# Four buffers instead of two and three between VectorE and the adding transfers of the last stage

## What is computed

```python
gate_scores = jax.nn.sigmoid(xf @ gate_w.T + balance_bias)
topk_scores, topk_idx = jax.lax.top_k(gate_scores, 2)          # 2 of 8 experts for each token
topk_scores = topk_scores / (topk_scores.sum(axis=-1, keepdims=True) + 1e-06)
comb = zeros((T, 8)).at[arange(T)[:, None], topk_idx].add(topk_scores)
h = jax.nn.silu(jnp.einsum('td,ehd->teh', xf, w1))              # 256 -> 512 for each expert
expert_out = jnp.einsum('teh,edh->ted', h, w2)                  # 512 -> 256
out = jnp.einsum('te,ted->td', comb, expert_out)                # weighted sum of two experts
```

## Time and profile before

| | |
|---|---|
| median of three runs | 3291.21 us (3287.84 to 3295.37) |
| the profiled execution | 3287.47 us |
| its span, first to last instruction | 3285.3 us |
| mean granted TensorE clock | 0.936 |
| busy share: TensorE, VectorE, ScalarE, GpSimd | 83%, 58%, 46%, 44% |
| the last stage | about 2958 to 3286 us |

### The profile page before, as it was taken

How to read it: one execution, slowest core, us unless ns; L and a number is a source line. 1 busy time by engine, 2 the same in 40 slices (tenths; PEclk the granted TensorE clock), 3 DMA queues, 4 the chain that set the end, 5 groups by cost and what they waited for, 6 DMA issues and landing times.

```text
span 3285.3 us, 49090 instructions
## 1 busy us (share of the span) xinstructions
PE 2739.6 (83%) x16588; PEld 1861.5 (57%) x16588; DVE 1904.1 (58%) x3444; ACT 1520.3 (46%) x2639; POOL 1452.9 (44%) x1633
## 2 busy tenths in 40 slices
PE   6888888857887888786999998799788888749997
PEld 2333333325564566533888875697555555537776
DVE  3888888866887688751222224402789998851111
ACT  4566665535775666410222210443666666522222
POOL 3666676654444577525000006300455555532333
PEclk8999999999998999988999999799999999869999
DMA  9600000000012000022566652100000000007675
GB/s 325 218 1 0 1 1 0 1 0 30 20 66 76 1 1 1 1 71 91 182 219 210 210 164 81 54 1 1 7 28 33 29 28 28 21 34 218 189 198 131
DMA packets 131956, 243.97 MB, mean 74 GB/s; under 512 B 15184, under 2 KB 103376, under 8 KB 121040
## 3 DMA queue, kind: packets, MB, share of 16 engines
q1 hardware_dynamic: 112320, 207.36, 19.4%
q0 software_dynamic: 19440, 34.10, 4.3%
HBM read 154.90 MB, written 87.43 MB: 74 GB/s over the span
## 4 chain that ended last, share of the span: by engine, by line
PE 24%; POOL 9%; issue 8%; DMA 7%; DVE 6%; ACT 2%; POOLq 1%; another core or an unknown queue 1%; SPq 0%; DVEq 0%; ACTq 0%
PE PS L2305 8%; DMA out<-f_y,f_token 6%; PE PS L1892 4%; PE PS L2261 4%; POOL e_hs L1451 2%; POOL rows_by_expert L2192 2%; POOL out L2621 1%; POOL e_qs L1454 1%; POOL rows_in_place L872 1%; PE PS L1306 1%; DVE e_mx L1354 1%; PE PS L1883 1%; PE PS L1249 1%; POOLq L2661 1%
## 5 line engine op out<-in xcount | busy, mean ns | idle before, releaser
L572 POOL TENSOR_TENSOR u_in<-dtx,b_rep 128x512 f32<-128x512 f32 x256 | 325.0, 1292 | 201.2 <-ACT b_rep L553 200.0
L588 DVE TENSOR_TENSOR_SCAN state<-PS,u_in 128x512 f32<-128x512 f32 x256 | 312.2, 1220 | 59.0 <-POOL u_in L572 34.8
L545 PE MATMUL PS<-scaled,ident 128*128 128x512 f32 x512 | 295.9, 662 | 28.2 <-DVE scaled L582 28.1
L2326 ACT ACTIVATE d_act_b<-PS 128x256 f32<-128x256 f32 (+2 forms) x192 | 76.1, 399 | 486.9 <-PE PS L2305 398.5
L1451 POOL TENSOR_TENSOR e_hs<-e_pr 128x512 f32<-128x512 f32 x128 | 162.7, 1271 | 231.0 <-ACT e_pr L1418 227.6
L2305 PE MATMUL PS<-d_unit_T,d_w 128*128 128x256 f32 (+1 forms) x1280 | 261.8, 358 | 1.0 <-ACT d_unit_T L2315 1.0
L2338 DVE TENSOR_TENSOR d_hid<-d_act_b,PS 128x256 f32<-128x256 f32 (+2 forms) x192 | 84.2, 440 | 295.9 <-ACT d_act_b L2326 276.5
L561 ACT ACTIVATE PS<-dt,decay_rate 128x508 f32<-128x508 f32 x256 | 173.5, 687 | 138.1 <-DVE state L588 136.4
L2305 PEld LDWEIGHTS PS<-d_unit_T,d_w 128*128 128x128 f32 x1280 | 222.0, 191 | 26.3 <-issue 1.4
L2621 POOL DMA_INDIRECT out<-f_y,f_token x71 | 110.2, 1553 | 218.8 <-DVE f_y L2612 160.8
L582 DVE TENSOR_TENSOR scaled<-state,PS 128x512 f32<-128x512 f32 x256 | 169.5, 665 | 55.5 <-PE PS L526 43.9
(11 more groups left out here) (451 smaller groups left out, 6477.0 us busy)
## 6 DMA issues: line engine op xcount, KB each, us to landing
d_w<-in_d_w SPq DMA_DIRECT2D x42, 1024.0 KB, 5.1
f_w<-in_f_w SPq DMA_DIRECT2D x40, 1024.0 KB, 5.1
rows_in_place<-blank SPq DMA_DIRECT2D x136, 272.0 KB, 5.0
d_w<-in_d_w SPq DMA_DIRECT2D x42, 512.0 KB, 4.0
rows_by_expert<-zeros SPq DMA_DIRECT2D x36, 256.0 KB, 2.6
f_unit_rows<-rows_in_place SPq DMA_DIRECT2D x31, 272.0 KB, 5.3
d_unit_rows<-rows_by_expert SPq DMA_DIRECT2D x31, 256.0 KB, 4.2
out_by_expert<-d_y_rows SPq DMA_DIRECT2D x31, 256.0 KB, 4.2
```

The source lines that it names most:

```text
L545: nc.tensor.matmul(YB[:, c], ident[:], scaled[:, (KD * n + c) % RC], start=False, stop=n == NS - 1).then_inc(m_y, 1)
L572: nc.gpsimd.tensor_tensor(u_in[:, k % RU], dtx[:, p, c], b_rep[:, n % RB], ALU.mult).then_inc(m_u, 1)
L588: nc.vector.tensor_tensor_scan(state[:, k % 2], DECAY[:, k % RD], u_in[:, k % RU], 0.0, ALU.mult, ALU.add).then_inc(m_h, 1)
```

## The change

`y` gets four buffers instead of two, and `token` four instead of three. The two waits on VectorE follow: both are now for the landing of unit u-4. The rings of rows and weights stay at three. No instruction is added or removed. Nothing else is touched.

```diff
--- before.py
+++ after.py
@@ -2498,7 +2498,7 @@
 
         FC, UT = 4, UR // 128
         UPS, WN = KD * 512, KD * 512 + 4 * D
-        RING = 3
+        RING, OUT = 3, 4
         mem = Stage(nc, sem_set[turn])
         t = lambda name, shape, dtype=F32: mem.take(f"{tag}_{name}", shape, dtype)
         s = lambda name: mem.sem(f"{tag}_{name}")
@@ -2508,8 +2508,8 @@
         rows = t("unit_rows", [128, RING, UT, ROW])
         xT = t("unit_T", [128, 2, KD, UR])
         hid = t("hid", [128, 2, FC, UR])
-        y = t("y", [128, 2, UT, D])
-        mine, share, token = t("mine_rows", [128, UT, E]), t("share_rows", [128, UT]), t("token", [128, RING, UT], I32)
+        y = t("y", [128, OUT, UT, D])
+        mine, share, token = t("mine_rows", [128, UT, E]), t("share_rows", [128, UT]), t("token", [128, OUT, UT], I32)
         UB = lambda f: PS[:, f, 0:UR]
         DB = lambda r: PS[:, 4 + r, 0:D]
         TB = PS[:, 6:8, 0:UR]
@@ -2601,15 +2601,15 @@
                 n = tiles[u]
                 nc.vector.tensor_tensor(mine[:, 0:n], rows[:, r, 0:n, D:D + E], table["mine"][:, u].unsqueeze(1).broadcast_to([128, n, E]),
                                         ALU.mult).then_inc(weighed, 1)
-                after(dve, added, 16 * late(u - RING + 1))
-                nc.vector.tensor_copy(token[:, r, 0:n], rows[:, r, 0:n, D + E]).then_inc(sent_to, 1)
+                after(dve, added, 16 * late(u - OUT + 1))
+                nc.vector.tensor_copy(token[:, u % OUT, 0:n], rows[:, r, 0:n, D + E]).then_inc(sent_to, 1)
                 dve.wait_ge(weighed, 2 * u + 1)
                 nc.vector.tensor_reduce(share[:, 0:n], mine[:, 0:n], AX.X, ALU.add).then_inc(weighed, 1)
                 dve.wait_ge(weighed, 2 * u + 2)
-                after(dve, added, 16 * late(u - 1))
+                after(dve, added, 16 * late(u - OUT + 1))
                 for k in range(n):
                     dve.wait_ge(down, upto[u] + k + 1)
-                    nc.vector.tensor_scalar(y[:, u % 2, k], DB(k), share[:, k:k + 1], None, ALU.mult).then_inc(mixed, 1)
+                    nc.vector.tensor_scalar(y[:, u % OUT, k], DB(k), share[:, k:k + 1], None, ALU.mult).then_inc(mixed, 1)
 
         def pool(pl):
             pl.wait_ge(stored, 16 * NG)
@@ -2618,7 +2618,7 @@
                 pl.wait_ge(sent_to, u + 1)
                 after(pl, added, 16 * upto[u])
                 for k in range(tiles[u]):
-                    nc.gpsimd.indirect_dma_start(tokens_of, bass.IndirectOffsetOnAxis(token[:, u % RING, k:k + 1], 0), y[:, u % 2, k], None,
+                    nc.gpsimd.indirect_dma_start(tokens_of, bass.IndirectOffsetOnAxis(token[:, u % OUT, k:k + 1], 0), y[:, u % OUT, k], None,
                                                  bounds_check=NG * GT - 1, oob_is_err=False, compute_op=ALU.add).then_inc(added, 16)
             pl.wait_ge(added, 16 * upto[SLOTS])
```

## The result

The changed kernel is slower: 3320.76 us (median of 4 runs, 3319.42 to 3337.45) against 3289.53 us for the kernel before (4 runs, 3280.98 to 3295.37). The ratio is 1.011, with a 95% interval of 1.008 to 1.014. The prediction was 3278 us, with a range from 3260 to 3297: the sign was wrong, and the time lies outside the range.

The account below looks back on a forecast made before the run. The prediction took the last stage's serial adding transfers, lengthened by weight loads, as the bound. Terms +3.7, -12.9 and -3.7 gave -12.9 us: 3287.47 to 3274.6, then 3.7 up to the runs' median, 3278; range 3260 to 3297.

Parts of the forecast that it names:

- The chain of landings: Last stage: each unit's adding transfers wait for the earlier landing; 0.86 us landing to issue, 1.86 more for two issues.
- The price list: GpSimd's transfers: a weight load lengthens a landing by its phase, +0.7 us at 2.8 ahead, +2.4 at 1.2 ahead.
- 164.6: Units 8 to 35: us the 21 double and 6 single units would take with no loads beside them.
- the 50.5 us: Units 8 to 35: remainder of 215.1 us beyond undisturbed transfers, claimed as the price of 27 weight loads, 1.87 each.
- the sum: Last stage: +3.7 us in units 8 to 12, -12.9 in units 12 to 33, -3.7 at the end; together -12.9.
- the forecast's own mechanism: Last stage: deeper y lets TensorE run further ahead, moving weight loads to cheaper phases of GpSimd's transfers; -12.9 us together.
- the half of periods in step: Units 12 to 33: half of some 22 loads fall at the cheap phase, 11 x (1.87 - 0.7) = -12.9 us.
- the distance of four: TensorE gets four units ahead of GpSimd, up from two, reached at output 17 and unit 13, where the gain begins.
- C: Slower: TensorE stands at its y gate before each unit, tying loads to landings; +18 us, 3309; chance 0.12.
- D: Deeper ring doesn't act: weight, hid or PSUM buffers hold TensorE at the same distance; 3291; with A 0.27.
- A: Nothing changes: every load crosses the chain somewhere and costs 1.87 us on average wherever it falls; 3291; with D 0.27.
- B: Full step: the odd periods fall into step as well, -31.6 us, some 3260; chance 0.06.

Follow-up runs that it names:

- y4_t5: Changed kernel with five token buffers instead of four, y still four: 3271.86 us, ratio 0.994 to the kernel before.
- paced_y2: Kernel before (y two, token three) plus a SyncE wait issuing the weights of unit u only after landing u-5: 3249.52 us, ratio 0.997 to before, same chip.
- y4_t3: Changed kernel with three token buffers instead of four, y still four: 3330.22 us, ratio 1.012 to the kernel before.
- y4_t5_splock: y4_t5 plus one SyncE wait holding rows of unit u, and weights behind them, until landing u-7: 3294.49 us, ratio 1.009 to the kernel before.
- y4_t4_wfirst: Changed kernel with SyncE issuing each unit's weights ahead of its rows: 3289.48 us, ratio 0.998 to the kernel before.

## Why the prediction was wrong

**What held.** The chain of landings bounds the stage in all kernels with loads: from unit 8 to unit 35 no step from landing to issue is above 0.9 us. That GpSimd doesn't wait for y, against the releaser in the trace, holds: with y written earlier or later, landing to issue is 0.85 us in the kernel after as well (3192.87 to 3193.72), and the second write of y ends only after that issue has begun. The price list was sound in its main point, that a load costs by its phase: 0.9 us each in y4_t5 (189.1 - 164.6 = 24.5 us for 26 loads), 1.87 before, 3.2 after. It was too sharp in its figures, each from one landing: with the load 2.5 us ahead the price is 1.3 in the mean of paced_y2 (5.1 against 3.81), not 0.7, and with nearly the same phase, 0.55 to 0.61 ahead, the kernel after has landings from 5.91 to 8.03. And the prices are not what leaving out the loads would give back: the kernels without loads take 182.1 us, not 164.6, as TensorE then bounds them. Of the 50.5 us, 3.5 are no time from last issue to landing but a stand of GpSimd between the two issues of unit 33 (last section), which the sum put to the loads. And the forecast's own mechanism works where it gets its premise. With the fifth token buffer the stretch is 26 us shorter, the ratio 0.994, some 21 us of the 3293.74; I had counted on 13. That the load then lies 2.4 to 3.3 us behind a last issue and not 2.8 ahead is a part that the prediction didn't foresee.

**The step that failed** is the first of the part-by-part: "In both kernels it costs nothing, covered by the y wait; behind it stand SyncE's rows of unit u+2 (line 2537), which then also come earlier." The numbers of the waits were right: after the change the cast waits for landing u-4, as y of u right behind it does. But the cover that mattered was not the y wait behind the cast, it was the one **ahead** of it. Before, y of u-1 had waited for the same landing u-3 and the cast never waited. After, y of u-1 waits for u-5 and the cast is the first to wait for u-4. So the cast became the instruction that all else hung on. I also named the wrong follower: `sent_to` for rows of u is tokens up to u-3, so the rows of unit u+3 hang on the cast of unit u, and with them, in the same queue, the weights of u+3. The premise "SyncE issues the load of unit v+3 when TensorE has finished output v" was then false, and everything after it with it: the sum, the half of periods in step, the distance of four.

**The rivals.** C had the right sign and about half of the size (+18 against 31), by another mechanism. It tied the loads to landings through TensorE's gate, with the load 1.8 us after the last issue, and y4_t3, y4_t5_splock and y4_t4_wfirst speak against that: the tie runs through SyncE's queue, and the load is 0.6 before. D said that something else might hold TensorE at the old distance; in fact something else, the weights, held it after the change. A's conserved excess is refuted by 0.9, 1.87 and 3.2 us a load, for 26 or 27 loads each. B's 3260 was not reached; the floor without loads is 33 us (182.1 against 215.1) below before, which is near B's 31.6.

**The two rules that were weighed.** The bubbles on TensorE (the Trainium skill, Perfetto Trace Analysis, Optimization Strategy) did point to buffers: y4_t5 is 26 us shorter in units 8 to 35, where the rule as I read it gave 25.2. That both numbers are alike does not make the reason the same, for eight buffers freed all bubbles and gave less. The even alternation between queues (the Trainium skill, DMA: Bandwidth & Descriptors, Queues, rings and completion order), taken as "a load costs the same at any phase", is not what the runs show; that was the prediction's reading of it, and the section itself gives no price.

## What to carry to other kernels

When a ring is deepened, write for each engine the list of waits in queue order, before and after, and mark the first that waits for each event: it is the wait **ahead** in the queue that covers another, and a wait that loses its cover takes everything that its semaphore feeds with it, through other queues too. Two buffers that are freed by the same event should not have the same depth if one is waited for earlier in the queue. Here the cast is covered where token has at least one buffer more than y; with four and four, and with four y and three token buffers, it isn't; one more token buffer, of two integers a partition, was worth 1.7%. Where short, serial transfers run beside large loads, look at when the loads are issued: the same 26 or 27 loads cost this stretch between 24 and 82 us.

## What was not expected of the hardware

From unit 12 to unit 32 the load of a double unit is 0.55 to 0.61 us ahead of the last issue, with one exception (0.23, unit 21), so a kernel can be locked into an expensive phase, the dearest that was seen here. A load in this phase is slowed as well, to 6.7 us from 5.1. And in every profile GpSimd stands for 2.7 to 6.6 us between the two issues of unit 33 without a releaser in the trace; between the two of the other units it is 0.30 to 0.37. After the change (the idle time in brackets, and the view of DMA issues from 3272.6 to 3272.9):

```profile
3272.51 1.55 POOL L2621 DMA_INDIRECT out<-f_y,f_token  x1 [6.89 <-DVE f_y L2612]
3280.17 1.55 POOL L2621 DMA_INDIRECT out<-f_y,f_token  x1 [6.11 <-issue]
```

```profile
out<-f_y,f_token POOLq DMA_INDIRECT x1, 7.2
```

It is 3.76 us before, 2.69 in y4_t5 and 3.13 without loads, and so 2.4 us of the loss. The traces say when it ends: the first transfer of the unit lands 7.2 us after its issue, at 3279.72, and the second issue follows 0.45 us later. In all 14 profiles it is 0.45 or 0.46 us from this landing to the second issue. So the stand follows the landing of the first transfer, which takes 7.2 us here and 4.2 in the two kernels without loads. Nothing in the kernel asks for this wait, and why it is there in this unit alone was not tried.
